# Macaron transformer on one core: the down projection waits for its two halves apart

## The reference, cut to what matters

```python
def _L0_ffn_ref(x, ...):            # 16 routed experts of width 64, and one shared
    h = jax.nn.silu(h1) * h3        # h1 = xf @ w1.T, h3 = xf @ w3.T, for each expert
    y = jnp.einsum('tei,edi,te->td', h, w2, comb)
...
def _L1_ffn_ref(x, ...):            # 8 experts of width 256
    h = jax.nn.silu(g) * u
    y = jnp.einsum('neh,edh->ned', h, w_down)
    out = jnp.einsum('ned,ne->nd', y, combine)
...
    x = x + 0.5 * _L0_ffn_ref(_layernorm(x, axis=-1), ...)
    x = x + _L0_attn_ref(_layernorm(x, axis=-1), ...)
    x = x + 0.5 * _L0_ffn_ref(_layernorm(x, axis=-1), ...)
    x = x + 0.5 * _L1_ffn_ref(_layernorm(x, axis=-1), ...)
    x = x + _L1_attn_ref(_layernorm(x, axis=-1), ...)
    x = x + 0.5 * _L1_ffn_ref(_layernorm(x, axis=-1), ...)
```

## Time and profile before

| | us |
|---|---|
| median of 3 runs | 1759.25 (1756.91 to 1759.9) |
| the profiled execution's own time | 1760.0 |
| its span, first to last instruction | 1756.7 |
| PE busy | 1628.4 (93% of the span) |
| DVE busy | 1272.1 (72%) |
| ACT busy | 1024.7 (58%) |
| POOL busy | 817.7 (47%) |

### The profile page before, as it was taken

One profiled execution on the slowest core, in us unless ns is written; L12 is line 12 of the kernel. 1 busy time (PEld: TensorE's weight loads), 2 busy tenths in 40 slices (PEclk: granted clock), 3 DMA queues, 4 the chain that ended last, 5 costly groups with the idle time before them and its releaser, 6 DMA issues. The chain is left out here.

```text
span 1756.7 us, 25930 instructions
## 1 busy us (share of the span) xinstructions
PE 1628.4 (93%) x8360; PEld 1157.5 (66%) x8360; DVE 1272.1 (72%) x3851; ACT 1024.7 (58%) x1734; POOL 817.7 (47%) x766
## 2 busy tenths in 40 slices
PE   5999879899999999997999999999998979999998
PEld 3777645555555555554777767777767867777776
DVE  6777658788778878864777867777766876777765
ACT  4666416666666676665666656555546655555554
POOL 2666611414332431321566656555574524555555
PEclk9999959999999999999999999999999999999999
DMA  4332111111111111101333341111200002111130
GB/s 150 98 98 85 64 33 35 21 21 26 25 30 21 26 26 29 25 7 42 106 113 111 95 142 49 49 49 50 79 18 1 1 12 86 55 55 61 56 96 19
DMA packets 58248, 95.03 MB, mean 54 GB/s; under 512 B 9312, under 2 KB 17120, under 8 KB 58112
## 3 DMA queue, kind: packets, MB, share of 16 engines
q1 hardware_dynamic: 56000, 91.07, 18.2%
q10 hardware_dynamic: 2112, 2.30, 0.4%
HBM read 76.76 MB, written 2.88 MB: 45 GB/s over the span
## 5 line engine op out<-in xcount | busy, mean ns | idle before, releaser
L697 DVE TENSOR_TENSOR big<-banks,big 128x512 f32<-128x512 f32 x384 | 264.5, 689 | 201.4 <-ACT banks L634 163.8
L1169 ACT ACTIVATE big<-banks 128x1024 f32<-128x1024 f32 (+3 forms) x384 | 301.6, 811 | 161.7 <-PE banks L1075 156.2
L634 ACT ACTIVATE banks<-banks 128x512 f32<-128x512 f32 x384 | 224.0, 583 | 276.3 <-PE banks L577 271.1
L707 DVE TENSOR_TENSOR big<-big,banks 128x512 f32<-128x512 f32 x400 | 274.9, 687 | 30.0 <-PE banks L580 16.9
L1056 PE MATMUL banks<-arena 128*128 128x512 f32 (+3 forms) x768 | 248.7, 401 | 21.2 <-DVE att_mx L1298 9.4
L1298 DVE CUSTOM_DVE_ANT_0 banks<-banks,att_mask 128x128 f32<-128x128 f32 (+3 forms) x512 | 234.3, 521 | 39.0 <-PE banks L1056 38.5
L1209 POOL TENSOR_SCALAR_AFFINE_SELECT big<-big 128x512 f32<-128x512 f32 x128 | 81.3, 635 | 355.4 <-ACT big L1169 355.4
L667 POOL TENSOR_TENSOR ffn1b_hid_l<-big,ffn1b_hid_h 128x512 fp32r<-128x512 f32 x128 | 165.4, 1292 | 128.5 <-ACT ffn1b_hid_h L639 128.5
L667 POOL TENSOR_TENSOR ffn1a_hid_l<-big,ffn1a_hid_h 128x512 fp32r<-128x512 f32 x128 | 165.3, 1291 | 116.6 <-ACT ffn1a_hid_h L639 116.6
L1075 PE MATMUL banks<-arena 128*128 128x512 f32 (+3 forms) x768 | 205.9, 354 | 12.1 <-ACT big L1169 12.0
L577 PE MATMUL banks<-xh,arena 128*128 128x512 f32 x512 | 208.0, 406 | 8.2 <-PEq L1465 6.8
(11 more groups left out here) (260 smaller groups left out, 3210.2 us busy)
## 6 DMA issues: line engine op xcount, KB each, us to landing
big<-weight_rows SPq DMA_DIRECT2D x256, 128.0 KB, 3.0
big<-weight_rows SPq DMA_DIRECT2D x128, 256.0 KB, 4.2
arena<-att_parts SPq DMA_DIRECT2D x16, 384.0 KB
arena<-att_parts SPq DMA_DIRECT2D x128, 48.0 KB
w_raw<-in_ffn_w_dram SPq DMA_DIRECT2D x12, 256.0 KB, 3.0
out_dram<-x SPq DMA_DIRECT2D x8, 256.0 KB, 2.3
setup_raw<-in_ffn_w_dram SPq DMA_DIRECT2D x3, 576.0 KB, 7.1
gau_angle<-in_consts_dram SPq DMA_DIRECT2D x2, 512.0 KB, 7.3
```

What stands on the lines that cost most here:

```text
L634: act.activation(gate if c < NSCALED else sil, gate, ACT.Silu).then_inc(silu_done, 1)
L697: dve.tensor_tensor(scl[:, num % 2, :], gate_ps[:, num % NB, :], share[:, c // PER, :], ALU.mult)\
L707: dve.tensor_tensor(hid[:, num % NH, :], scl[:, num % 2, :] if c < NSCALED else sil, up_ps[:, num % NB, :], ALU.mult).then_inc(hidden, 1)
L1169: act.activation(probs[:, unit % NPROB, 2 * pair:2 * pair + 2, 0:c], score_ps[:, pair, :, 0:c], ACT.Exp, scale=SCALE).then_inc(exped, 1)
```

## The change

The single wait before the three products of `project` is split: the first two products wait until `hid_h` is written, the third until `hid_l` is. No instruction is added, removed or moved to another place.

```diff
@@ project(g, c), on PE
                 if c == 0:
                     at_least(pe, y_out, g)
-                pe.wait_ge(low_cut, num + 1)
+                pe.wait_ge(high_cut, num + 1)
                 pe.matmul(y_ps, down_h[:, ws], hid_h[:, num % NH, :], start=c == 0, stop=False)
                 pe.matmul(y_ps, down_l[:, ws], hid_h[:, num % NH, :], start=False, stop=False)
+                pe.wait_ge(low_cut, num + 1)
                 pe.matmul(y_ps, down_h[:, ws], hid_l[:, num % NH, :], start=False, stop=c == NC - 1)\
                     .then_inc(down_done, 1)
```

## The result

The changed kernel takes 1732.03 us (median of 4 runs, 1730.6 to 1733.0), the kernel before beside it 1758.08: a ratio of 0.9851, 95% interval [0.9834, 0.9868], 26 us faster. The forecast was 1731, in a range from 1719 to 1746. The profiled execution took 1731.65 us, its span 1729.9, against 1760.0 and 1756.7.

The account below looks back on a forecast made before the run. PE was taken as the bound, busy 93% of 1756.7 us. Gains of 12.0 + 10.8 + 6.4 = 29.2 us from 1760.0 gave 1730.8, or 1730.1 from the runs' median, stated as 1731, range 1719 to 1746.

Parts of the forecast that it names:

- The sum: Whole kernel: gains of 12.0 us in ffn1a, 10.8 in ffn1b and 6.4 in layer 0, together 29.2 us.
- Where PE loses: Expert passes: PE idles before L589 until POOL's `low`, and restarts late; 67.1 us in four passes, all the change can touch.
- The slower case: Rival, all 400 chunks: third product's weights can't load ahead of its wait, 44 us lost against 29 gained, 1774; chance 0.04.
- Layer 1: ffn1a and ffn1b: stalls start from PE's own matmuls, so the gain is kept, 12.0 and 10.8 us.
- chunk 12: Layer 1, six times a pass: the 0.54 us stall exceeds 0.46, leaving 0.16 with a 0.08 restart, 1.0 us a pass.
- The tail: Last two chunks of ffn1b: third product starts 0.57 us earlier, of 2.3 held there; 1.75 left.
- Layer 0: ffn0a and ffn0b: the chain is not PE's, so only 3.2 us a pass is gained, 6.4 for both.
- the loop: Layer 0, first share to next: DVE's run, `combt`, store and shares hold each group; only 0.26 us gained as `combt` starts earlier.
- The first group of ffn0b: First group of a layer 0 pass: `combt` waits longer for PE there, so 0.6 us gained.
- the share of the two passes: ffn0a and ffn0b alike: 0.6 in the first group, 1.6 in the next six, 1.0 in the last two chunks: 3.2 us.
- The clock: Rival: a lower-clock stretch, seen at attention's start, is spared or brought to another tail; 5 us gained or lost, no chance given.

Follow-up runs that it names:

- e3_second_waits_low: Against the changed kernel, only the first product goes ahead of the low part; the second and third wait for it: 1742.75 us, 0.9903 of the kernel before.

## Why the prediction was right

**The number.** The sum promised 29.2 us and the change gave 26. That 1731 lies only 1 us from the measured 1732.03 is in part luck: the forecast was rounded up by 0.9 us, and the kernel before ran 1.2 us faster beside the changed one than the median it started from. These two closed 2 of the 3 us.

**Where PE loses.** The idle time and the long L589 were the stalls, and they went as one: PE idles 0.0 us before L589 in layer 1 now. The third product needs no more than a satisfied wait: 0.23 us behind L590 wherever `low` is done. The trace agrees with the rule that the prediction took from the Trainium skill ("TensorE: Matmul & The Clock Gate", Part 2), that weight loads are pulled ahead of running matmuls, also for a wait in the middle of an accumulation once it is met: a third product's weights load from 1606.79 in ffn1b, as the second product starts, and its matmul follows at 1607.02. The slower case, which needed 0.073 us a chunk, did not come.

**Layer 1** was forecast at 12.0 and 10.8 us; the passes gave 11.4 and 9.9, and the layer alone 23 in the runs. The stalls below 0.46 us went whole; chunk 12 kept 0.16 and its restart of 0.11, 0.27 together against the 0.16 that I had allowed. I had taken 0.08 where 0.16 stands, and for the restart 0.08 where 0.11 stands. That is 0.7 of the missing 0.9 us in ffn1b. The tail came as worked out: two lines of ffn1b's last chunk after, beside the earlier trace rows:

```profile
1723.29 1.27 POOL L668 TENSOR_TENSOR ffn1b_hid_l<-big,ffn1b_hid_h 128x512 fp32r<-128x512 f32 x1 [0.29 <-ACT ffn1b_hid_h L640]
...
1724.62 0.50 PE L592 MATMUL banks<-ffn1b_hid_l,arena 128*128 128x512 f32 x1 [0.60 <-POOL ffn1b_hid_l L668]
```

The third product starts 1.33 us behind the start of `low`, where L591 started 1.90 behind it: 0.57.

**Layer 0** is where the reason was right and its size too large: 6.4 forecast, 5.6 in the two traces, 4.2 in the runs of the layer alone. `combt` came 0.26 to 0.29 us earlier behind `high` in each of the six middle groups of ffn0b, as worked out. In ffn0b's groups that can hardly be seen, for the rest of the loop isn't fixed: from the end of `combt` to the start of `scale` it was 5.12 to 5.35 us in these groups before and 4.97 to 6.02 after, 0.8 us more in sum. The change need not be the cause of that: in the kernel with layer 1 alone, whose layer 0 has the single wait, the same six times are 5.20 to 5.88 us and 1.4 more in sum than before. The first group of ffn0b gained nothing in this trace, where 0.6 was expected, but took 22.22 us in the second profile of the changed kernel, against 23.02 before. That the loop holds is shown by two experiments from opposite sides: with all waits on the low part gone from the middle groups they stayed at 22.95 us, and with the loop shortened they fell to 22.4.

What the forecast had wrong is the share of the two passes, 3.2 us each. From the first product of ffn0a to the first of ffn0b it is 796.8 us before and 798.5 with layer 1 alone, against 793.4 to 794.5 in three profiles with the split in layer 0. From there to the first product of ffn1a it is 188.4 and 190.8 against 188.7, 189.3 and 190.1: of a gain in ffn0b nothing can be told by the time ffn1a starts.

**The clock** took part of it. Its rival had 5 us gained or lost by a stretch at the lower clock; what came is smaller and at another place. PE's matmuls ahead of ffn1a's first product are 0.43 us apart in the changed kernel's profile, and that boundary is 2.1 us longer. Over all thirteen profiles it follows the granted clock of the 10 us from ffn0b's last product: 7.9 to 8.2 us long at 1.00, 9.3 to 10.0 at 0.83 and 10.5 to 11.2 at 0.66. The four kernels with the single wait in ffn0b's last chunks had 1.00 or 0.83, the nine profiles with another wait there 0.83 or 0.66. Whether the shorter tail makes the low clock more likely stays open, since both kinds vary.

The gated stage, the same instructions everywhere, took 139.6 to 142.6 us in the thirteen profiles. The kernel before was near the top and the changed one at the bottom, which the two spans compared above count as 3.0 us of gain; what makes the stage vary is not shown. The sum of the parts, 29.2 us, exceeds the measured 26 by the 1.5 of layer 1, the 0.8 of layer 0 and such differences between the passes.

## What to carry to other kernels

Put each wait on the first instruction that needs it: with operands that come in two parts, the products of the early part are slack for the late one, 0.23 us each here, and a wait that was met cost nothing (0.23 us from start to start). Before counting a stall as a gain, follow its chain back to where it starts: here the stalls that began with PE's own work were gained for good, and those inside a loop of other engines and transfers came back as another wait, but for what the loop itself got shorter. When such a loop is cut, look for the next one at once, since it sets the gain, as the add and the selection did here.

## What the runs showed of the hardware

A stall on PE costs more than its gap: at full clock the matmul behind the one that waited starts 0.30 to 0.34 us later instead of 0.23, wherever the wait sits: before the first product (the kernel before), the second (`e3_second_waits_low`) or the third (the changed kernel). Over the 10 us behind the tails of ffn0b and ffn1a the granted clock was anything from 0.55 to 1.00, in kernels with and without the split wait. It differed between two profiles of the same kernel too (0.66 and 0.83 after ffn0b), and none of these runs tells why. Behind ffn0b it went with 3 us of time: 7.9 us of boundary at 1.00, 11.2 at 0.66.
